# Rounding in an eight-core gated-attention and ternary-FFN kernel: a chain of SBUF comparisons in place of the PSUM chain with clamping

## The reference

```python
x = layernorm(x + attn(x))        # attn: three projections, gates, a linear scan over tokens, a fourth projection
x = layernorm(x + ffn(x))

def ffn(x):                       # W_g, W_u: 8192 x 2048, W_d: 2048 x 8192
    xq = activation_quant(rms_norm(x))
    g = silu(xq @ sign(W_g).T)
    u = xq @ sign(W_u).T
    return (g * u) @ sign(W_d).T

def activation_quant(x):
    s = 127.0 / max(abs(x), axis=-1)
    return clip(round(s * x), -128, 127) / s
```

## Time and profile before

| | |
|---|---|
| median of 3 runs | 3137.3 us (3130.86 to 3201.54) |
| the profiled execution | 3139.62 us |
| its span, first to last instruction of the slowest core (core 3) | 3137.7 us |
| spans of the 8 cores | 3106.3 to 3137.7 us |
| TensorE busy | 2091.0 us, 67% |
| VectorE busy | 737.1 us, 23% |
| ScalarE busy | 847.9 us, 27% |

### The profile page before, as it was taken

How to read it: one execution, slowest core, us unless ns; L and a number is a source line. 1 busy time by engine, 2 the same in 40 slices (tenths; PEclk the granted TensorE clock), 3 DMA queues, 4 the chain that set the end, 5 groups by cost and what they waited for, 6 DMA issues and landing times. The chain is left out here.

```text
span 3137.7 us, 22259 instructions; the slowest of 8 cores (3106.3 to 3137.7 us)
## 1 busy us (share of the span) xinstructions
PE 2091.0 (67%) x9116; PEld 914.6 (29%) x9116; DVE 737.1 (23%) x662; ACT 847.9 (27%) x778; POOL 6.4 (0%) x14
## 2 busy tenths in 40 slices
PE   0882870775067531100989989898998989899836
PEld 0432430222022200000434434343443434344303
DVE  2001232000311257685011120210202011020242
ACT  1115654111310111111332223223131332314016
POOL 0000000000000000000000000000000000000000
PEclk9995885777588655555989999998999989999955
DMA  9215005101320020002352334435242453324122
GB/s 290 87 46 169 1 1 174 40 0 52 122 81 27 0 107 0 0 0 80 135 201 97 118 109 147 173 108 178 77 174 108 128 194 108 137 99 169 39 107 108
DMA packets 96981, 312.93 MB, mean 100 GB/s; under 512 B 5105, under 2 KB 5234, under 8 KB 79474
## 3 DMA queue, kind: packets, MB, share of 16 engines
q1 hardware_dynamic: 93650, 294.74, 27.5%
q0 software_dynamic: 3232, 16.78, 1.4%
HBM read 294.73 MB, written 16.78 MB: 99 GB/s over the span
## 5 line engine op out<-in xcount | busy, mean ns | idle before, releaser
L656 PE MATMUL PS<-B,SGN 128*128 128x512 bf16 x1024 | 389.8, 381 | 185.3 <-ACT SGN L639 185.3
L736 PE MATMUL PS<-PB,SGN 128*128 128x512 bf16 x1024 | 398.7, 389 | 82.8 <-ACT SGN L721 82.8
L691 PE MATMUL PS<-B,SGN 128*128 128x512 bf16 x1024 | 398.4, 389 | 49.9 <-ACT SGN L676 49.9
L693 PE MATMUL PS<-B,SGN 128*128 128x512 bf16 x1024 | 398.3, 389 | 0.0
L738 PE MATMUL PS<-PB,SGN 128*128 128x512 bf16 x1024 | 397.9, 389 | 0.0
L234 PE MATMUL PS<-B,WR 128*128 128x512 bf16 x768 | 320.0, 417 | 107.0 <-ACT WR L217 91.6
L658 PE MATMUL PS<-B,SGN 128*128 128x512 bf16 x1024 | 389.7, 381 | 0.0
L236 PE MATMUL PS<-B,WR 128*128 128x512 bf16 x768 | 318.5, 415 | 0.0
L749 DVE TENSOR_TENSOR XF<-XF,PS 128x1024 f32<-128x1024 f32 x112 | 136.8, 1221 | 337.3 <-PE PS L738 337.3
L699 DVE TENSOR_TENSOR PB<-SCRA,PS 128x1024 bf16<-128x1024 f32 x32 | 39.1, 1221 | 718.1 <-PE PS L693 681.5
L664 ACT ACTIVATE SCRA<-PS 128x1024 f32<-128x1024 f32 x32 | 32.8, 1024 | 640.7 <-PE PS L658 640.7
(11 more groups left out here) (122 smaller groups left out, 1711.4 us busy)
## 6 DMA issues: line engine op xcount, KB each, us to landing
STG<-wgq SPq DMA_DIRECT2D x64, 1024.0 KB, 7.0
STG<-wuq SPq DMA_DIRECT2D x64, 1024.0 KB, 7.2
STG<-wdt SPq DMA_DIRECT2D x64, 1024.0 KB, 6.6
STG<-xt SPq DMA_DIRECT2D x16, 1024.0 KB, 7.8
STG<-wft SPq DMA_DIRECT2D x16, 1024.0 KB, 8.0
STG<-wit SPq DMA_DIRECT2D x16, 1024.0 KB, 8.2
STG<-wgt SPq DMA_DIRECT2D x16, 1024.0 KB, 7.6
STG<-wot SPq DMA_DIRECT2D x16, 1024.0 KB, 7.8
```

The lines of the kernel that those rows point to most:

```text
L656: e.matmul(PS[psg][:, 0:512], lhsT, b1(dc)[:, 0:512], start=st, stop=sp)
L691: e.matmul(PS[psu][:, 0:512], lhsT, b1(dc)[:, 0:512], start=st, stop=sp)
L693: inst = e.matmul(PS[psu][:, 512:1024], lhsT, b1(dc)[:, 512:1024], start=st, stop=sp)
L736: e.matmul(PS[psi][:, 0:512], lhsT, pb(k)[:, 0:512], start=st, stop=sp)
```

## The change

After the conversion by ScalarE, the five operations of VectorE are replaced by eight: the difference now goes to `scra(1)` in SBUF, six comparisons follow (with -0.5, 0.5, -1.5, 1.5, -2.5 and 2.5), each of which reads the difference and `scra(0)` and overwrites `scra(0)` with the outcome minus what was there, and a plain multiplication by PS[3] writes `b1(dc)`. After an even number of turned signs the result is the converted value plus one for each upper threshold reached and minus one for each lower one. The clamping to -128 and 127 is gone. Each of the eight waits for the operation before it.

```diff
-            op("vector", lambda e: e.tensor_sub(PS[1][:], PS[0][:], scra(0)),
-               inc=("ve", 1),
-               waits=[("se", cnt("se"))] + (mm_waits(1, []) if dc == 0 else []))
-            op("vector", lambda e: e.scalar_tensor_tensor(
-                scra(0), PS[1][:], 0.5, scra(0), ALU.is_ge, ALU.add),
-                inc=("ve", 1), waits=[("ve", cnt("ve"))])
-            op("vector", lambda e: e.scalar_tensor_tensor(
-                PS[0][:], PS[1][:], -0.5, scra(0), ALU.is_le, ALU.subtract),
-                inc=("ve", 1), waits=[("ve", cnt("ve"))])
-            op("vector", lambda e: e.tensor_scalar(
-                scra(0), PS[0][:], -1.0, 127.0, ALU.mult, ALU.min), inc=("ve", 1),
-                waits=[("ve", cnt("ve"))])
-            op("vector", lambda e, dc=dc: e.scalar_tensor_tensor(
-                b1(dc), scra(0), -128.0, PS[3][:], ALU.max, ALU.mult),
-                inc=("ve", 1), waits=[("ve", cnt("ve"))])
+            op("vector", lambda e: e.tensor_sub(scra(1), PS[0][:], scra(0)),
+               inc=("ve", 1), waits=[("se", cnt("se"))])
+            for thr in (-0.5, 0.5, -1.5, 1.5, -2.5, 2.5):
+                alu = ALU.is_le if thr < 0 else ALU.is_ge
+                op("vector", lambda e, thr=thr, alu=alu: e.scalar_tensor_tensor(
+                    scra(0), scra(1), thr, scra(0), alu, ALU.subtract),
+                    inc=("ve", 1), waits=[("ve", cnt("ve"))])
+            op("vector", lambda e, dc=dc: e.tensor_mul(b1(dc), scra(0), PS[3][:]),
+               inc=("ve", 1), waits=[("ve", cnt("ve"))])
```

## The result

The changed kernel takes 3199.22 us at the median of 10 runs, against 3136.45 us for the kernel before measured beside it. The ratio is 1.0202, with a 95% interval of 1.0191 to 1.0213. The forecast was 3201 us and a ratio of 1.0203. The number lies 0.02 points above the bound of 2% that the prediction named, and the interval reaches to both sides of it, so these runs don't settle on which side the change falls.

The account below looks back on a forecast made before the run. VectorE's quantisation loop, with TensorE idle, was taken to bound the kernel. 16 passes at 3.95 us more each give 63.2 us, with 0.4 us for stalls 63.6; 3137.3 + 63.6 = 3200.9, about 3201 us, range 3186 to 3211 us.

Parts of the forecast that it names:

- The loop is alone on the path: Quantisation loop: only VectorE works while TensorE waits, no slack beside it, so each added microsecond delays the first matmul equally.
- The size of a step: Loop: start-to-start step of a waiting VectorE instruction, 1.325 us; seven replace four, 9.28 against 5.33 us a pass.
- The total: Whole kernel: the loop adds 63.6 us to the 3137.3 us median, giving about 3201 us.
- Stalls: Loop: single stalls of about 0.5 us, valued in proportion to the 48 added instructions, some 0.4 us.
- Seam and FFN: Behind the loop: the 20 us to the first matmul and the FFN keep their length; TensorE's longer idling costs nothing.
- Rival A: Loop: six SBUF-only comparisons run at the cast's 0.69 us, saving 51.8 us, a time of 3149; chance 0.05.
- Rival B: Loop: without a PSUM operand the next comparison starts after 1.14 us, saving 18 us, giving 3183; chance 0.06.
- Rival C: Seam behind the loop: loads or signs start while VectorE still rounds, at most 20 us go, giving 3181; chance 0.02.
- Rival D: Loop or FFN: 0.46 us stalls in each pass, or a less favourable FFN phase; 7 us more, 3208; chance 0.08.
- The Trainium skill's rule: Loop: a semaphore between VectorE operations costs nothing extra, pricing 48 steps at 1.14 us, 54.7 us, a time of 3192.
- The chances: Whole kernel: slower by over 2% 0.56, within 2% 0.43, faster 0.01; the forecast itself 0.78.

Follow-up runs that it names:

- two-block run: The changed kernel with two of the 16 blocks worked through alternately, each VectorE instruction waiting for the last but one; 3152.12 us, ratio to before 1.0046.

## Why the prediction was right

- **The loop is alone on the path.** Right, and now shown from four sides: work added (the change), removed (two comparisons, two instructions), moved out of the loop (no cost in the FFN) and reordered inside it all came out at the end as the step sums had it, each ratio within 0.002 of the one expected.
- **The size of a step.** I took 1.325 us; measured are 1.329 between comparisons, 1.33 over all seven. Ranging it by L482 in the earlier trace rows and by the four present steps in the earlier trace rows was enough. My reason for going under 1.33, that the instructions which write PSUM are followed later by 0.01 to 0.02 us, holds in a smaller size: over the 16 passes the step behind L583 averages 1.338 us with the difference in PSUM and 1.329 with it in SBUF, which the single passes shown above cannot tell apart. It is no general rule of PSUM, as L576 writes PSUM too and is followed after 1.327 us. The pass comes to 14.25 us where the sum had 14.20.
- **The total.** +63.6 us forecast for the loop, 63.1 us measured in it and 62.8 us between the medians. Stalls: the waits in the loop of the changed kernel list one of 0.5 us at L587, where the earlier trace rows has two, so the 0.4 us that I added for more of them were not needed. Two small errors cancel in the sum: the steps were 0.004 us too short, 0.45 us over 112 of them, and the stalls 0.4 us too many. That the forecast lies in the middle of the measured interval, which is 7 us wide, is luck in its last microsecond or two.
- **Seam and FFN.** The seam stayed at 20.9 us against 20.2, and the granted clock at 0.50 through both stretches, the 1.2 GHz level. The longer idling of TensorE had no price: its matmuls take 0.38 us again from 1550.10, 2.9 us after the first, which is sooner than the 6 us of the earlier trace rows. No run shows why it was sooner.
- **Rival A** (comparisons at the cast's rate) fell on 1225 ns in the changed kernel's own trace. **Rival B** fell in its place, as the step is 1.33 us, but its size exists: 1.135 us is what a step takes when the direct predecessor isn't waited for. **Rival C** did not happen, and its price was tested: with the loads really ahead, 8 of the 20 us go. **Rival D** had no stalls to show.
- **The Trainium skill's rule** ("VectorE: DVE Perf Modes", "The DRAIN you can't avoid") is that a semaphore between VectorE operations costs nothing extra. By the two-block run this is half right here: a wait on the last but one is free at 1.135 us a step, a wait on the last one costs 0.19 us. Pricing the added steps by it would have given 3192 us, 7 us too low.
- **The chances.** The margin to 2% was 0.9 us in my sum, and the measured ratio has 1.0191 to 1.0213 as its interval. Which side of the bound it falls on was not to be known from the trace, and the measurement doesn't settle it either.

## What to carry to other kernels

Before pricing an edit, find out whether anything runs beside it: a stage in which every other engine shows 0 charges each instruction its full start-to-start step, whatever the engine's share of the span. Count steps and not durations; a chain in which each instruction waits for the one in front pays for the hand-over each time, and two independent blocks worked through alternately get it back without removing an instruction. And first ask if the stage's instructions are needed at all: the best version here drops eight of ten of VectorE's, with the clamping and ScalarE's conversion.

## What was unexpected of the hardware

Waiting for the direct predecessor is what makes VectorE's step 1.33 us; a wait that is one instruction older leaves it at 1.135 us. The other surprise is how free the types are: a multiplication that writes int32 from bf16 and f32 sources, and one that reads int32 and writes bf16, both take 1.22 us at 128x1024, the same as the f32 forms. Where the difference lies, PSUM or SBUF, did not change the comparison by a nanosecond (1225 and 1225).
